# A fused 1x1-convolution attention layer on one core: all tasks in a new order, odd high halves on ScalarE, weights in three chains

## What is computed

```python
wp = normalize_weight(w_proj)[:, :, 0, 0] / fan_in      # w / (eps + alpha * |w|), per row
wo = normalize_weight(w_out)[:, :, 0, 0] / fan_in
h = jnp.einsum('oc,bcn->bno', wp, xf)                    # b 16, c 512, n 1024, o 1536
q, k, v = jnp.split(h.reshape(B, N, n_heads, 3 * d_k), 3, axis=-1)
q = pixnorm(q) * scale; k = pixnorm(k) * scale; v = pixnorm(v)
attn = jax.nn.softmax(jnp.einsum('bihd,bjhd->bijh', q, k), axis=2)
res = jnp.einsum('bijh,bjhd->bihd', attn, v).reshape(B, N, C)
res = jnp.einsum('oc,bnc->bon', wo, res).reshape(B, C, H, W)
return (a_c * x + b_c * res) / div
```

## Time and profile before

| | us |
|---|---|
| median of 3 runs | 3233.88 |
| lowest, highest | 3227.86, 3242.86 |
| the profiled execution, its own time | 3256.49 |
| its span, first to last instruction | 3254.4 |
| mean granted TensorE clock | 0.983 of full speed |
| PE, PE weight load, DVE, ACT busy | 3027.5, 2060.7, 2666.0, 2304.7 |
| DMA queue's share of 16 engines | 28.0% |

### The profile page before, as it was taken

The page is one execution under the profiler, slowest core; times in us unless marked ns, Lnnn a source line. Parts: engine busy times, 40 slices in busy tenths (PEclk is TensorE's granted clock), DMA queues, the critical chain, the costliest instruction groups (busy, mean ns, idle before and its releaser), DMA issues.

```text
span 3254.4 us, 91845 instructions
## 1 busy us (share of the span) xinstructions
PE 3027.5 (93%) x36928; PEld 2060.7 (63%) x36928; DVE 2666.0 (82%) x3295; ACT 2304.7 (71%) x2865; POOL 335.8 (10%) x678
## 2 busy tenths in 40 slices
PE   4899999999999899999989999899999999999987
PEld 3666666766667566666666667566665666667653
DVE  3788787888879888797888878788897887878875
ACT  4677676767767777676777767677776776767664
POOL 0120100201102011100201002011010201002010
PEclk9999999999999999999999999999999999999999
DMA  2312323124142321323223232231423223232232
GB/s 78 62 42 49 90 48 92 41 60 94 36 102 44 80 63 38 102 48 83 49 57 90 43 99 36 69 81 35 108 40 83 57 48 91 48 92 41 50 79 59
DMA packets 459635, 212.11 MB, mean 65 GB/s; under 512 B 407953, under 2 KB 407953, under 8 KB 459153
## 3 DMA queue, kind: packets, MB, share of 16 engines
q1 hardware_dynamic: 459152, 205.58, 28.0%
HBM read 71.30 MB, written 33.55 MB: 32 GB/s over the span
## 4 chain that ended last, share of the span: by engine, by line
issue 77%; POOL 10%; PE 5%; DVE 5%; ACT 1%; DMA 1%; POOLq 1%; SPq 0%; DVEq 0%; ACTq 0%
POOL rs L323 3%; POOL rs_t L319 2%; POOL rs_t L317 2%; POOL rs_t L321 2%; DVE probs L628 2%; PE ps_pv L799 1%; DVE probs L619 1%; PE ps_dense L758 1%; PE ps_score L778 1%; PE ps_dense L762 1%; PE ps_dense L760 1%; POOL sumsq L314 1%; ACT e_tile L456 1%; DVE arena L590 0%; ACT probs L463 0%
## 5 line engine op out<-in xcount | busy, mean ns | idle before, releaser
L456 ACT ACTIVATE e_tile<-ps_score,shift 128x1024 f32<-128x1024 f32 x1024 | 1109.3, 1113 | 316.3 <-PE ps_score L778 183.2
L628 DVE TENSOR_TENSOR probs<-e_tile,probs 128x1024 f16<-128x1024 f32 x1024 | 1242.0, 1226 | 56.4 <-ACT probs L463 47.1
L799 PEld LDWEIGHTS ps_pv<-v_pair,probs 128*128 128x128 f16 x24576 | 804.2, 98 | 297.8 <-DVE probs L628 145.6
L799 PE MATMUL ps_pv<-v_pair,probs 128*128 128x65 f16 (+1 forms) x24576 | 863.1, 194 | 119.6 <-DVE probs L628 87.6
L778 PE MATMUL ps_score<-qkT 64*128 64x512 f16 x6144 | 762.1, 381 | 6.8 <-ACT e_tile L456 3.9
L619 DVE CAST probs<-e_tile 128x1024 f16<-128x1024 f32 x640 | 442.2, 693 | 247.2 <-ACT e_tile L456 241.4
L758 PE MATMUL ps_dense<-wpT_hi,x_hi 128*128 128x512 f32 x1536 | 629.9, 410 | 8.4 <-DVE x_lo L557 7.0
L762 PE MATMUL ps_dense<-wpT_hi,x_lo 128*128 128x512 f32 x1536 | 601.9, 392 | 0.0
L760 PE MATMUL ps_dense<-wpT_lo,x_hi 128*128 128x512 f32 x1536 | 600.2, 391 | 0.0
L778 PEld LDWEIGHTS ps_score<-qkT 64*128 64x128 f16 x6144 | 257.6, 95 | 312.7 <-issue 42.6
L416 ACT ACTIVATE squares<-ps_dense 128x512 f32<-128x512 f32 x384 | 228.1, 594 | 277.4 <-PE ps_dense L762 277.4
(11 more groups left out here) (50 smaller groups left out, 1765.7 us busy)
## 6 DMA issues: line engine op xcount, KB each, us to landing
x_raw<-in_x SPq DMA_DIRECT2D x128, 256.0 KB, 3.0
x_res<-in_x SPq DMA_DIRECT2D x128, 256.0 KB, 2.7
out<-x_res SPq DMA_DIRECT2D x128, 256.0 KB, 2.5
arena<-in_w_proj SPq DMA_DIRECT2D x24, 128.0 KB, 2.6
qkT<-arena SPq DMA_TRANSPOSE x128, 4.3
resT<-res_split SPq DMA_TRANSPOSE x128, 3.1
arena<-in_w_out SPq DMA_DIRECT2D x1, 1024.0 KB, 5.7
```

The costliest lines, as they stand in the source:

```text
L456: act.activation(e_tile[:, t % 2, :, :], ps_score[:, t % 2, :, :], ACT.Exp, bias=shift[:, 0:1], scale=1.0 / (QK_UP * QK_UP)).then_inc(exp_ ...
L628: dve.tensor_tensor(probs_of(b, t, 1), e_tile[:, t % 2, :, :], probs_of(b, t, 0), ALU.subtract).then_inc(probs_low, 1)
L799: mm = pe.matmul(ps_pv[:, h, o:o + n], probs_of(b, t, part)[:, h, queries], v[:, cols], start=(j == 0 and it == 0 and part == 0 and cols.s ...
```

## The change

- `ACT_HIGH` becomes (1, 3, 5, 7): ACT rounds four of eight high halves in place of three.
- All tables are new; with them the order on every engine. Banks too.
- The high and low halves of one slot can now be far apart in a queue, and `pv_done` counts slots (64 an image) instead of pairs (32).
- Image 0 has tables of its own for what lies ahead of it (`FIRST_...`), with the weights' steps among them (`W_...`): loads, squares, halves, and norms in three chains of tiles 0 to 3, 4 to 7 and 8 to 15 (`W_CHAINS`). Turning goes through four buffers. Waits are added for what the order no longer gives: a first projection waits for the low halves of its weight tiles, a first copy into `arena` for the tile it overwrites, the first score for all 16 tiles.

```diff
-ACT_HIGH = (1, 4, 6)
+ACT_HIGH = (1, 3, 5, 7)
+W_CHAINS = ((0, 4), (4, 8), (8, 16))
...
-PROJ_BANK = (0, 1, 0, 1, 0, 1, 0, 1, 0, 1, 0, 1, 0, 1, 0, 1, 0, 1, 0, 1, 0, 1, 0, 1)
-OUT_BANK = (1, 0, 1, 0, 0, 1, 0, 1)
+PROJ_BANK = (1, 0, 1, 0, 1, 0, 1, 0, 1, 0, 1, 0, 1, 0, 1, 0, 1, 0, 0, 1, 1, 0, 1, 0)
+OUT_BANK = (1, 0, 1, 0, 1, 0, 0, 1)
...
-            body(-1, prev=False, cur=False)
+            for s in range(-span, 0):
+                task(0, s, opening)
             body(0, prev=False)
...
+        def turned_of(m):
+            return ps_score[:, m // 2 % 2, m % 2, :].rearrange("p (t o) -> p t o", o=P)
...
             def copy_proj(b, n):
+                if first(b, n >= RING):
+                    act.wait_ge(w_turned, n + 1)
...
-                after(act, pv_done, VISITS * b + (t - PROB_BUFS) // 2 + 1)
+                after(act, pv_done, SLOTS * b + t + 1 - PROB_BUFS)
...
             def project(b, n):
+                if first(b, nt):
+                    pe.wait_ge(w_low, GROUP_UNITS * (g + 1))
...
             def score(b, m):
+                if first(b, m):
+                    pe.wait_ge(w_low, W_TILES)
...
-                mm.then_inc(pv_done, 1)
+                    mm.then_inc(pv_done, 1)
...
+            def turn_weights(m):
+                pe.wait_ge(w_scaled, m + 1)
+                after(pe, w_low, m - 3)
```

## The result

The changed kernel takes 3129.49 us, the median of 4 runs (3127.34 to 3131.56), against 3231.79 us before (4 runs): ratio 0.9678 [0.9652, 0.9704]. The forecast was 3046 us with a range of 3010 to 3125. The sign was right, the gain was little more than half: -102 us between medians where -188 was forecast, and -126 between the two profiled spans (3254.4 and 3128.4), to which the prediction's sum was made.

The account below looks back on a forecast made before the run. Bound by order, not work: PE loses 12.8 us of each 196.55 us image. Opening -25, image 0 -12, fourteen images -134, image 15 -17 sum to -188 us, giving 3046 us; range 3010 to 3125.

Parts of the forecast that it names:

- part 4: Waits added to a steady image: 1.2 us for x_res, 1.4 not followed, 2.6 together; image 187.0 us, bounds 184.5 and 193.
- The nominal image: Steady image in the new order if PE never waited: 184.4 us, against 183.8 us of work in the old order.
- step (b): Attends waiting for DVE's low half of the probabilities: 87.6 us in 126 waits, the largest at the seam between images.
- part 1: New order of dense groups: at the seam low half 63 ends near T+5.0, PE reaches attend 31 at T+5.9, no wait.
- cumulated work leaves room: Argument against queue-head slips: DVE's cumulated work never falls over 3 us behind PE's in the new list.
- Part 2: Every second high half on ACT: a pair of slots takes about 3.5 us in place of 4.55 without dense groups.
- part 6: Image 0 takes 166 us against 177.9; image 15 takes 167 against 184.15, with 4.0 us a pair.
- Part 5: Opening, weights in three chains: projection 0 starts at 22 us, score 0 near 81, a gain of 25 us.
- Rival B: Heads of the in-order ACT, DVE and SP queues slip 1 to 2 us: image 192 us, 3116 us; chance 0.22.
- Rival C: Short idles in the new order lower PE's clock in steady images: +45 us, 3091 us; chance 0.07.
- D: Steady image stays at 196.55 us and only the ends gain: 3180 us; chance 0.05.
- E: Slower: score 0 waits for late transposes of qkT; 16 us an image would give 3286 us; chance 0.04.

Follow-up runs that it names:

- part 2 alone: Kernel before, old order and tables kept, with ACT rounding high halves of slots 1, 3, 5, 7 in place of 1, 4, 6: 3226.51 us, ratio 0.9934.
- 8 to 128 waits: Changed kernel with 8, 32, 64 or 128 already fulfilled semaphore waits on PE ahead of its loop: 3073.76, 3072.25, 3081.76 and 3085.6 us.
- 512 waits: Changed kernel with 512 already fulfilled semaphore waits (256 instructions) on PE ahead of its loop: 3158.74 us.

## Why the prediction was wrong, point by point

- **The failed step is the last term of part 4**, "for what I did not follow (the loop's seam, the DMA's spread) 1.4 us". It measured 8.3 us at each of 13 seams, 7.7 us an image: PE's jump back with its block fetches, 6.5 us, and the lower clock behind them, 1.8. The other term of the 2.6 us was too high in turn: x_res 1.2 us by the walk, 0.2 by the rows (3.0 us in 10 waits), 0.5 in the kernel without PE's loop. The nominal image and the seams alone, 184.4 + 13 x 8.3 / 14, give the 192.1 that were measured.
- **Behind it stands a reading**: step (b) put the 2.70 us of attend 31 down to DVE, because the wait named DVE's low half. The jump of 3.6 us fell in the same place and ended last at all 13 seams. Without the jump attend 31 still waits 1.1 us there, and the image gains nothing, so the old order's loss to DVE was real but was not this wait alone. The walk of the seam in part 1 (T+5.0 and T+5.9, "no wait") was right on the data and had no row for PE's own sequencer. The upper bound of 193 in part 4 held the truth, but for another reason ("half of the loss stays"), and the range's end of 3125 was set by the rivals and not by it.
- **The nominal image, 184.4 us, was right**: 184.0 to 185.5 with PE's loop gone. (For the old order the six neighbours at 0.14 give 184.0 and not 183.8; nothing hangs on it.) So were "cumulated work leaves room" and the banks: waits for copies went from 44.2 to 3.5 us.
- **Part 2** was right in size: the pair 3.61 us (forecast "about 3.5") in place of 4.55, and 3.62 in the last image of the changed kernel, where part 6 had taken 4.0. Image 15 gained 21 us (17), of which part 2 alone brings 9.
- **Part 5** was right: projection 0 at 21.2 (22), score 0 at 75.0 (81); the interleaving carries most of it. Its terms add up to 84 and not 81 (22 + 40 + 12 + 5 + 4.6), so the walk was 9 us too slow.
- **Rival B** gave 3116, close to the measured time, and 192 us an image, by a mechanism that isn't there: its closeness is luck. **Rival C** fell: the order cycles through the banks of PSUM with hardly an idle moment and runs at a granted clock of 1.00 for 2583 us; the rule of the Trainium skill that was weighed (TensorE: Matmul & The Clock Gate, "A second HAM failure mode: psum-queue depth-cycling") has no case in these runs. The lower clock stood behind the long idle stretch of each seam, 13 x 1.8 = 23 us. Behind the stretches of 3.1 to 3.7 us of the kernels with 8 to 128 waits it stood in 24 of 52 cases. **D** and **E** fell: the images changed, and score 0 doesn't wait for qkT in the loop.

## What to carry to other kernels

A wait that names an engine ends with it, but something else may have been running as long underneath: before the gain of a better order is booked, ask what else lies in that idle time, and read the sequencer's branches at the loop's edge as well. In a loop whose body is long on one engine, either write that engine's stream out (here 110 us) or cut the loop where the engine has work queued (here 95 us). When a kernel changes by a few microseconds an iteration for no reason in its data flow, count the instruction packets for each jump.

## What the runs showed of the hardware

- PE's jump back takes 3.6 us (3.3 to 4.9 over all runs), the fall-through 83 ns; DVE's and ACT's take 63 and 45 ns in the same loop. With all engines written out the second instruction queue, q14, has 87 packets in place of 167. The 80 fewer would fit some 2 for each of 13 jumps of ACT, DVE and POOL; nothing in their branches shows such a fetch.
- A loop that begins within one instruction or so of the end of a 16 KB block pays a second fetch of 3.0 us at every jump; with 17 instructions left, PE does them and then waits. Shifts of 0.25 to 8 KB avoid it, 16 KB brings it back (one run each; 4 to 128 instructions and 256). Two kernels with the same work and order thus differ by 56 us (3129.49 and 3073.76) through four instructions ahead of the loop: 13 x 3.1 = 41 us of idle time and 8 x 1.8 = 14 us for the clock at eight seams.
- Behind idle stretches of 5.9 to 6.8 us (the changed kernel and 512 waits) score 0 had the lower clock at all 26 seams, behind 3.1 to 3.7 us (8 to 128 waits) at 24 of 52.
- PE has work queued behind its sequencer: of a branch with a median of 3.85 us only 1.05 is seen at one cut of the loop, of one of 3.55 us 3.3 at another.
- Each extra semaphore wait on PE ahead of the loop costs about 0.1 us by the instruction: image 0 grows from 168 us (4 instructions) to 195 (256).
